# Two attentions in one kernel: the norms between them by groups of four tiles, and the second part's first-layer weights prepared inside the first attention

## What is computed

```
def core(x):                                   # x: (2, 1024, 128)
    x0 = layernorm(x)                          # norm 0
    a  = local_attention_1(x0)                 # 16 heads of 8, keys i-32..i, biases; one layer
    x  = x + layernorm(a)                      # norm 1 and the sum
    y  = layernorm(x)                          # norm 2
    for l in range(6):                         # 16 heads of 64, window 32, rotary tables
        y = y + attn_layer(shift(y), Wqkv[l], q_scale[l], k_scale[l], Wo[l])
        y = y + ffn_layer(shift(y), W1[l], W2[l])   # norm, gated GELU, hidden size 341
    return x + layernorm(y)                    # norm 3 and the last sum
```

## Time and profile before

| | |
|---|---|
| median of three executions | 2151.84 us (2143.28 to 2152.09) |
| profiled execution, its own time | 2149.59 us |
| span of its trace | 2147.8 us |
| busy share: TensorE, VectorE, ScalarE, GpSimd | 90%, 78%, 75%, 77% |
| opening, start of the span to the first attention | 24.2 us |
| first attention | 140.2 us |
| between it and the layers | 37.7 us |
| layers, up to the last `hidden` | 1921.0 us |
| from there to the end | 24.7 us |

### The profile page before, as it was taken

The page is one execution under the profiler, slowest core; times in us unless marked ns, Lnnn a source line. Parts: engine busy times, 40 slices in busy tenths (PEclk is TensorE's granted clock), DMA queues, the critical chain, the costliest instruction groups (busy, mean ns, idle before and its releaser), DMA issues.

```text
span 2147.8 us, 67396 instructions
## 1 busy us (share of the span) xinstructions
PE 1932.7 (90%) x22192; PEld 1460.9 (68%) x22192; DVE 1676.1 (78%) x4006; ACT 1604.5 (75%) x5607; POOL 1662.5 (77%) x1251
## 2 busy tenths in 40 slices
PE   5992999998999988999988999988999988999986
PEld 3761777774777774777774777774777774777772
DVE  4666888886888876888876888876888876988865
ACT  4872888884888874888884888874888885888872
POOL 2124999985999976899976899976899976999960
PEclk9995999999999999999999999999999999999998
DMA  2001321110311111211111211111211111112210
GB/s 63 13 12 50 82 55 44 44 45 25 88 44 44 44 45 38 76 44 44 44 45 41 74 44 44 44 45 42 73 44 44 44 45 35 46 44 49 54 28 20
DMA packets 44547, 99.43 MB, mean 46 GB/s; under 512 B 7344, under 2 KB 24208, under 8 KB 43504
## 3 DMA queue, kind: packets, MB, share of 16 engines
q1 hardware_dynamic: 44400, 97.59, 17.8%
HBM read 19.59 MB, written 1.05 MB: 10 GB/s over the span
## 4 chain that ended last, share of the span: by engine, by line
PE 27%; DVE 26%; issue 18%; ACT 18%; POOL 8%; DVEq 1%; POOLq 0%; ACTq 0%; DMA 0%; SPq 0%
ACT prob L485 10%; DVE n2c L791 6%; DVE n L784 5%; DVE ts_ L794 5%; ACT nat L501 4%; PE bank L1115 3%; PE bank L1149 3%; DVE tc_ L787 3%; DVE nmax L741 3%; PE bank L1122 3%; ACT kT L523 2%; PE bank L1151 2%; PE bank L1150 2%; POOL rn L319 2%; POOL ropeL L356 2%
## 5 line engine op out<-in xcount | busy, mean ns | idle before, releaser
L319 POOL TENSOR_TENSOR rn<-n2c,half_neg 128x8 f32<-128x8 f32 x384 | 632.8, 1648 | 129.5 <-DVE n2c L791 128.7
L485 ACT ACTIVATE prob<-bank,nmax 128x96 f32<-128x96 f32 x1536 | 504.1, 352 | 131.0 <-DVE nmax L741 130.8
L321 POOL TENSOR_TENSOR tsum<-tc_,ts_ 128x512 f32<-128x512 f32 x384 | 489.9, 1276 | 0.0
L324 POOL TENSOR_TENSOR w_nat<-tsum,rn 128x512 f32<-128x512 f32 x384 | 400.6, 1043 | 37.8 <-POOL tsum L321 15.1
L784 DVE TENSOR_REDUCE n<-nat 128x8 f32<-128x512 f32 x384 | 262.5, 683 | 140.9 <-ACT nat L501 138.2
L485 ACT ACTIVATION_READ_ACCUMULATOR prob<-bank,nmax 128x1 f32 x1536 | 334.3, 218 | 0.0
L1149 PE MATMUL bank<-w_hi,xs 128*128 128x512 f32 x576 | 277.0, 481 | 34.2 <-DVE ts_ L794 13.1
L494 ACT ACTIVATE pT<-bank 96x512 f32<-96x512 f32 x384 | 231.3, 602 | 74.4 <-PE bank L1122 72.3
L501 ACT ACTIVATE nat<-bank 128x512 f32<-128x512 f32 x384 | 233.0, 607 | 72.0 <-PE bank L1151 69.4
L794 DVE TENSOR_TENSOR ts_<-bank,ropeL 128x256 f32<-128x256 f32 x768 | 285.8, 412 | 0.0
L1122 PE MATMUL bank<-idf,prob 128*96 128x128 f32 x1536 | 244.9, 282 | 43.6 <-ACT kT L523 29.5
(11 more groups left out here) (125 smaller groups left out, 3413.7 us busy)
## 6 DMA issues: line engine op xcount, KB each, us to landing
vspace<-v_nat SPq DMA_DIRECT2D x96, 384.0 KB, 4.0
vspace<-v_nat SPq DMA_DIRECT2D x96, 256.0 KB, 3.4
vspace<-v_nat SPq DMA_DIRECT2D x95, 128.0 KB, 2.3
nat<-w_qkv SPq DMA_DIRECT2D x5, 1536.0 KB, 8.5
wo<-w_o SPq DMA_DIRECT2D x6, 512.0 KB, 4.0
w<-w SPq DMA_DIRECT2D x6, 341.0 KB, 3.0
shared<-w_qkv SPq DMA_DIRECT2D x1, 1536.0 KB, 6.8
w<-w SPq DMA_DIRECT2D x6, 192.0 KB, 3.0
```

Source lines behind the costliest of these rows:

```text
L319: nc.gpsimd.tensor_tensor(rn[:, r, :], n2c[:, r, :], half_neg[:, 0:8], ALU.pow).then_inc(pool_step, 1)
L321: nc.gpsimd.tensor_tensor(tsum[:, r, :], tc_[:, r, :], ts_[:, r, :], ALU.add).then_inc(pool_step, 1)
L324: nc.gpsimd.tensor_tensor(w_nat[:, r, :].rearrange("p (h d) -> p h d", d=D), tsum[:, r, :].rearrange("p (h d) -> p h d", d=D), rn[:, r, :] ...
L485: last = nc.scalar.activation(prob[:, 4 * b + i, :], SB[b][:, i * SPAN:(i + 1) * SPAN], ACT.Exp, bias=nmax[:, p, 8 * G + 4 * b + i:8 * G + ...
```

## The change

The four norms outside the layers are taken group by group. VectorE's part is split into `moments` (four `bn_stats`), `deviations` (four `bn_aggr`, and the addition) and `normalise` (four `tensor_scalar`), and GpSimd takes a power of four columns a group (`pow_norm`). The normalising of a group stands behind the next group's moments. TensorE transposes a group as soon as it is normalised. Each group of `x` has a semaphore of its own. The memsets have another order, with the four powers of norm 0 among them.

In the first attention VectorE takes the `bn_stats` of tile n - 1 inside tile n. SyncE issues layer 0's five weight loads before the attention. ScalarE does the three pieces of `split` in tiles 0, 1 and 14; GpSimd makes the four tables behind the keys of tiles 3, 5, 7 and 9, and two pieces of `rest` behind tiles 11 and 13 and the third after tile 15; its loop over tiles is written out.

At the end TensorE transposes groups 0 and 1 of the result before `down(3)`, VectorE takes their moments before `output(3)`, and the rest follows group by group.

```diff
-                              ).then_inc(x_loaded, 16)
+                              ).then_inc(x_in[s], 16)
...
+                    eng.dma_start(wqkv0, Wqkv[l, :, :]).then_inc(qkv_loaded, 16)
+                    eng.dma_start(wo[:, :, :], Wo[l, :, :].rearrange("(i p) c -> p i c", p=P)).then_inc(wo_loaded, 16)
+                    eng.dma_start(w1[:, :], W1[l, :, :]).then_inc(ffn_loaded, 16)
+                    eng.dma_start(w2[:, :, :], W2[l, :, :].rearrange("(i p) c -> p i c", p=P)).then_inc(ffn_loaded, 16)
+                    eng.dma_start(vec[:, :], par[l, :, :]).then_inc(ffn_loaded, 16)
...
-                    eng.wait_ge(phase, 4 * 2)
-                    eng.dma_start(wqkv0, Wqkv[l, :, :]).then_inc(qkv_loaded, 16)
...
+            def pow_norm(k, g):
+
+                eng.wait_ge(n_eps, k * SUPERS + g + 1)
+                nc.gpsimd.tensor_tensor(rstd[:, g * SUPER:(g + 1) * SUPER], veps[:, g * SUPER:(g + 1) * SUPER],
+                                        half_neg[:, 0:SUPER], ALU.pow).then_inc(n_pow, 1)
...
             nc.gpsimd.memset(half_neg[:, :], -0.5).then_inc(init_done, 1)
-            nc.gpsimd.memset(w_nat[:, :, :], 0.0).then_inc(init_done, 1)
-            nc.gpsimd.memset(kT[:, :, :, :], 0.0).then_inc(init_done, 1)
+            nc.gpsimd.memset(follows[:, :], 1.0).then_inc(init_done, 1)
             nc.gpsimd.memset(vw1[0:WIN, 0, 0, :], 0.0).then_inc(init_done, 1)
             nc.gpsimd.memset(xA[:, :, :], 0.0).then_inc(init_done, 1)
+            eng.wait_ge(init_done, 4)
+            nc.gpsimd.memset(follows[:, 0:TILES:PER_SEQ], 0.0).then_inc(init_done, 1)
+            pow_norm(0, 0)
+            pow_norm(0, 1)
+            nc.gpsimd.memset(kT[:, :, :, :], 0.0).then_inc(init_done, 1)
+            pow_norm(0, 2)
+            pow_norm(0, 3)
             nc.gpsimd.memset(xB[:, :, :], 0.0).then_inc(init_done, 1)
-            nc.gpsimd.memset(follows[:, :], 1.0).then_inc(init_done, 1)
-            eng.wait_ge(init_done, 7)
-            nc.gpsimd.memset(follows[:, 0:TILES:PER_SEQ], 0.0).then_inc(init_done, 1)
+            nc.gpsimd.memset(w_nat[:, :, :], 0.0).then_inc(init_done, 1)
             eng.wait_ge(init_done, 8)
-
-            def pow_rstd(k):
-
-                eng.wait_ge(ln_step, 2 * k + 1)
-                nc.gpsimd.tensor_tensor(rstd[:, :], veps[:, :], half_neg[:, :], ALU.pow).then_inc(ln_pow, 1)
 
             def rotate(q_idx):
...
-            pow_rstd(0)
...
-            split_keys(0, 0)
-            split_keys(1, 1)
-            with eng.Fori(1, TILES // 2) as i:
-                split_keys(i * 2, 0)
-                split_keys(i * 2 + 1, 1)
...
-            eng.wait_ge(c_loaded, CONSTS)
-            tables(0)
+
+            for t in range(TILES):
+                split_keys(t, t % 2)
+                if t in (3, 5, 7, 9):
+                    table(0, (t - 3) // 2)
+                if t in (11, 13):
+                    rest(0, (t - 11) // 2, True)
+            rest(0, 2, True)
             end(eng)
 
             begin(eng, 2)
-            pow_rstd(1)
-            rest(0, 0, True)
-            rest(0, 1, True)
-            pow_rstd(2)
-            rest(0, 2, True)
+            for k in (1, 2):
+                for g in range(SUPERS):
...
-            pow_rstd(3)
+            for g in range(SUPERS):
+                pow_norm(3, g)
...
                 if ahead:
                     qkv_first(t + 2, p)
                     copy_first(n + 3, 1 - p)
+                if isinstance(n, int) and n in (0, 1, TILES - 2):
+                    split(0, min(n, 2), True)
                 if not opening:
...
-            for k in range(3):
-                split(0, k, True)
...
+            def settle(last):
+
+                last.then_inc(n_step, 1)
+                steps[0] += 1
+                eng.wait_ge(n_step, steps[0])
...
+            def moments(src, g):
+                for n in range(g * SUPER, (g + 1) * SUPER):
                     last = nc.vector.bn_stats(stats[:, n, :], src[:, n, :])
-                last.then_inc(f_st, 1)
...
+            def deviations(g):
+                for n in range(g * SUPER, (g + 1) * SUPER):
                     last = nc.vector.bn_aggr(mv[:, n, :], stats[:, n, :])
-                last.then_inc(f_st, 1)
-                eng.wait_ge(f_st, fst[0])
-                fst[0] += 1
...
+            def normalise(src, k, g):
+                eng.wait_ge(n_pow, k * SUPERS + g + 1)
...
-            eng.wait_ge(x_loaded, 16 * SUPERS)
-            norms(x_nat, 0)
+            for g in range(SUPERS):
+                eng.wait_ge(x_in[g], 16)
+                moments(x_nat, g)
+                deviations(g)
+                if g:
+                    normalise(x_nat, 0, g - 1).then_inc(n_norm, 1)
+            normalise(x_nat, 0, SUPERS - 1).then_inc(n_norm, 1)
...
+                if not opening:
+                    eng.wait_ge(a_y, t)
+                    nc.vector.bn_stats(stats[:, n - 1, :], y_nat[:, n - 1, :])
...
+                eng.wait_ge(a_y, t + 1)
+                settle(nc.vector.bn_stats(stats[:, n, :], y_nat[:, n, :]))
...
-            norms(y_nat, 1)
-            eng.wait_ge(ln_step, 4)
-            nc.vector.tensor_tensor(x_nat[:, :, :], x_nat[:, :, :], ln_nat[:, :, :], ALU.add).then_inc(f_st, 1)
-            eng.wait_ge(f_st, fst[0])
-            fst[0] += 1
-            norms(x_nat, 2)
...
+            def add_up(g):
+
+                g4 = slice(g * SUPER, (g + 1) * SUPER)
+                settle(normalise(y_nat, 1, g))
+                settle(nc.vector.tensor_tensor(x_nat[:, g4, :], x_nat[:, g4, :], ln_nat[:, g4, :], ALU.add))
+                moments(x_nat, g)
+                deviations(g)
+
+            for g in range(SUPERS):
+                deviations(g)
+            for g in range(SUPERS):
+                add_up(g)
+                if g:
+                    normalise(x_nat, 2, g - 1).then_inc(n_norm, 1)
+            normalise(x_nat, 2, SUPERS - 1).then_inc(n_norm, 1)
             end(eng)
...
+            def final_moments(g):
+                eng.wait_ge(lnT_free, g + 1)
+                moments(y_nat, g)
+                deviations(g)
+
...
+                    if s == 3 and last:
+                        for g in range(2):
+                            final_moments(g)
...
+            def final_sum(g):
+                g4 = slice(g * SUPER, (g + 1) * SUPER)
+                settle(normalise(y_nat, 3, g))
+                nc.vector.tensor_tensor(x_nat[:, g4, :], x_nat[:, g4, :], ln_nat[:, g4, :], ALU.add).then_inc(out_ready, 1)
+
+            final_moments(2)
+            final_sum(0)
+            final_moments(3)
+            for g in range(1, SUPERS):
+                final_sum(g)
...
+            def transpose_norms(k):
+                for g in range(SUPERS):
+                    eng.wait_ge(n_norm, k * SUPERS + g + 1)
+                    transposes(lambda n: ln_nat[:, n, :], g)
+
+            def transpose_result(g):
+                eng.wait_ge(f_out, (DEPTH - 1) * SUPERS + g + 1)
+                transposes(lambda n: xA[:, n, 1:P + 1], g)
...
+                    elif last:
+                        transpose_result(0)
+                        transpose_result(1)
...
-            eng.wait_ge(f_out, DEPTH * SUPERS)
-            transposes(lambda n: xA[:, n, 1:P + 1], 2)
+            transpose_result(2)
+            transpose_result(3)
```

More of the change, by code:

```diff
@@ L973, in _ @@
             layers(eng, layer)
-            eng.wait_ge(lnT_free, SUPERS)
-            for n in range(TILES):
-                last = nc.vector.bn_stats(stats[:, n, :], y_nat[:, n, :])
-            last.then_inc(f_st, 1)
-            at = base_st + DEPTH * SUPERS
-            eng.wait_ge(f_st, at + 1)
-            for n in range(TILES):
-                last = nc.vector.bn_aggr(mv[:, n, :], stats[:, n, :])
-            last.then_inc(f_st, 1)
-            eng.wait_ge(f_st, at + 2)
-            nc.vector.tensor_scalar(veps[:, :], mv[:, :, 1], EPS, None, ALU.add).then_inc(ln_step, 1)
@@ L986, in _ @@
-            eng.wait_ge(ln_pow, 4)
-            for n in range(TILES):
-                last = nc.vector.tensor_scalar(ln_nat[:, n, :], y_nat[:, n, :], mv[:, n, 0:1], rstd[:, n:n + 1],
-                                               ALU.subtract, ALU.mult)
-            last.then_inc(f_st, 1)
-            eng.wait_ge(f_st, at + 3)
-            for s in range(SUPERS):
-                t4 = slice(s * SUPER, (s + 1) * SUPER)
-                nc.vector.tensor_tensor(x_nat[:, t4, :], x_nat[:, t4, :], ln_nat[:, t4, :], ALU.add).then_inc(out_ready, 1)
+            def final_sum(g):
+                g4 = slice(g * SUPER, (g + 1) * SUPER)
+                settle(normalise(y_nat, 3, g))
+                nc.vector.tensor_tensor(x_nat[:, g4, :], x_nat[:, g4, :], ln_nat[:, g4, :], ALU.add).then_inc(out_ready, 1)
@@ L997, in _, with transposes @@
+            final_moments(2)
[3 more added lines that the diff above has]
+                final_sum(g)
         @block.tensor
         def _(eng):
```

(12 more changed lines are left out.)

47 lines of the change are left out of this document (21 added, 26 removed).

## The result

The median after the change is 2129.93 us (2125.49 to 2131.05, five executions), against 2151.84 before. After over before is 0.990, with the interval 0.988 to 0.992: faster by 1.0%, where 2130.1 was forecast. The profiled execution took 2130.22 us with a span of 2128.4; before it was 2149.59 and 2147.8.

A forecast was written before the change was run, and what follows sets the result against it. The short stages were read as chains with one engine working at a time, most time lying in the untouched layers. Gains 3.3 - 1.3 + 13.1 + 6.6 = 21.7 us, from 2151.84 to 2130.1, range 2120 to 2140.

The forecast's parts named there:

- the table load starts at 16.6: Opening: ScalarE's table load waits for all eight memsets and starts at 16.6 instead of 19.87 us, gain 3.3 us.
- its lower end of 0: Opening: gain of 0 if the weight loads issued behind the constants delay these, for which TensorE waits.
- Tile 1's piece costs its full 0.96: First attention: split's piece in tile 1 stands right before ScalarE's copy of the heads, without slack, costing 0.96 us.
- Tiles 0 and 14: nothing: First attention: split's pieces cost 0, tile 14 having 1.63 us idle, tile 0 no such copy; tile 0's upper end 0.96.
- `bn_stats` fills the 0.27 us: First attention: VectorE's bn_stats, 0.22 us, fits its 0.27 us idle before a tile's third evacuation; 0.3 us in all.
- GpSimd's tables and SyncE's issues: nothing: First attention: tables and rest fit GpSimd's 6.63 us before the next keys, SyncE's issues precede the value moves; cost 0.
- the last power is not covered: 1.1: Between attention and layers: VectorE waits 1.1 us for GpSimd's last power before the last normalising.
- Rival 1: GpSimd's power also holds the port, so normalisings between and in the closing wait: 5 us less, 2135.1 us; chance 0.12.
- Rival 2: Moved work costs more: late constants, no opening gain, attention losing its upper bound of 3.5 us; 2135.6 us, chance 0.13.
- Rivals 3 and 4: GpSimd's pieces delay attention keys, 2146.4 us, chance 0.04; bn_stats makes VectorE the attention's bound, 2166.4 us, chance 0.02.
- the last store behind it stays: Closing: the last store after VectorE's last sum stays as before, within a gain of 6.6 us.
- the last store goes alone: Closing: upper end of the gain, 7.5 us, if the last store goes alone.

The follow-up runs named there:

- e8_between: Changed kernel with weight loads, split, tables and rest back where they stood before, norms by groups kept; median 2131.32 us, 0.9905 of before.
- e2_behind: Changed kernel with tile 1's piece of split moved behind ScalarE's copy of the heads; attention 140.78 us, one execution 2124.90 us.
- e1_late: Changed kernel with split's second and third pieces in tiles 14 and 15, second rest behind tile 15; attention 140.92 us, median 2124.24 us, 0.9896 of before.
- e3_half: Changed kernel with only half of split's second piece in tile 1, the other half in tile 15, second rest behind tile 15; attention 147.17 us, 2127.59 us.
- e5_memsets: Changed kernel with the memsets of xB and w_nat moved behind tile 1's keys; opening 18.82 us, one execution 2133.9 us.
- e9_best: Changed kernel with split pieces in tiles 14 and 15, identity's own semaphore, xB and w_nat memsets behind tile 1's keys, vspace memset before the powers; 2122.41 us.
- e6_idf: Changed kernel with TensorE's first transposes waiting for the identity alone, by its own semaphore; opening 19.00 us, one execution 2125.96 us.
- e7_idf_mem: Changed kernel with the identity's own semaphore and the xB and w_nat memsets behind tile 1's keys; opening 16.37 us, one execution 2120.36 us.

## Why the prediction was right, and where it was not

**The frame held.** The reading that the short stages are chains in which one engine works at a time on all 16 tiles was right, and it carries the result: the two stages that were counted along VectorE's chain gave 23.1 us, and 19.7 were forecast. `e8_between` shows that the groups bring it. The total of 21.7 was 2.3 above the 19.4 of the profiles, within 0.2 us of the difference of the medians. That closeness is luck in part: +1.1, -3.2, +1.9, -3.6 and +1.5 cancel.

**The opening** gained 4.4 instead of 3.3, by another path than the one argued. The step "the table load starts at 16.6", behind the eighth memset, failed: it started at 15.50, before that memset's end, and in `e2_behind` at 14.07. Only the first copy waits (15.79 there). So the load and the wait overlap, and by the memset alone the stage would end at 16.0 + 3.1 = 19.1. But in this profile another wait ended last, TensorE's for the constants: 14.30 + 5.5 = 19.8. The text had named late constants as its lower end of 0, and TensorE waiting for them as a sign of being wrong; that wait came, 1.9 us later than before in this profile, and cost 0.7. The hold by GpSimd's memset of `kT`, set at 0.7, is there (1.07 us for `veps`).

**The first attention** cost 4.5 instead of 1.3, outside the given 3.5. The terms one by one:
- *Tile 1's piece costs its full 0.96*: that held, 0.95 us in front of the copy of the heads and 1.09 of TensorE's idle time in front of the projection, and none in `e2_behind`. What the sum left out is what TensorE does behind the wait: the clock fell to 1.2 GHz and stayed there for about 6.8 us, with 32 small matmuls at 1.88 us that take 1.11 at the full clock. That is a term of its own, 3.03 us, put at nothing without being named. Both together are 3.98.
- *Tiles 0 and 14: nothing.* Tile 14 took 7.16 us from the copy of the heads ahead of its piece to the copy behind it, and 7.17 before. For tile 0 no cost shows: from the attention's start to the values of tile 1 it took 20.99 us, 0.65 less than before, and 20.88 in `e8_between`, without the piece. But this stretch varies by more than that with the clock.
- *`bn_stats` fills the 0.27 us*: it takes 0.28 in front of the third evacuation, and the eleven tiles in the middle took 86.79 us instead of 86.42. That is 0.03 each, 0.4 in all where 0.3 was forecast.
- *The end* took 0.8 more from tile 15's copy of the heads on. It does so too in `e2_behind` and `e8_between` (8.72 and 8.86 us, against 7.80 before), but not in `e1_late` (7.84). At this end TensorE's clock goes down in all kernels as its work runs out, and the sooner it does so behind that copy, the longer the step, in all twelve profiles: 8.88 us with the fall 0.5 us behind the copy (`e3_half`), 8.58 with 0.9 (after), 8.17 with 1.4 (`e5_memsets`), 7.80 with 1.9 (before) and 7.58 with 2.2 (`e9_best`). So these 0.8 us are a price of the clock too. What moves the fall was not tried.
- *GpSimd's tables and SyncE's issues: nothing.* Confirmed: the keys came in time, and `e1_late` with all transfers in place took 140.92 us, where `e8_between`, without them, took 140.80; the eleven tiles in the middle took 86.76 and 86.77. So the weights' transfers do not slow the attention.

Added up: 0.95 and 3.03 in tile 1, 0.4 in the middle and 0.8 at the end, less 0.65 at the start, are the 4.5.

How far the fall of the clock follows from the piece: it fell behind tile 1 in five of seven profiles with a piece or half of one in front of the copy, and in none of five without. In the two exceptions (`e6_idf`, `e7_idf_mem`) TensorE was as idle, and the clock stayed. The windows of `e7_idf_mem`:

```profile
38.00:40.00 2.00, 0.92 (x10) 0.28 (x6) 0.43 (x1) 2.00 (x7) 2.00 (x2) 1.00 0.18 41
40.00:44.00 4.00, 4.00 (x60) 3.52 (x59) 3.14 (x7) 4.00 (x27) 0.57 (x1) 1.00 0.02 4
```

and its timeline:

```profile
37.99 0.28 ACT L471 ACTIVATE v_nat<-bank 128x128 f32<-128x128 f32 x1 [1.34 <-DMA vspace<-v_nat]
...
39.81 0.46 PE L1099 MATMUL bank<-vspace,oT 128*128 128x128 f32 x2 [1.08 <-ACT oT L487]
...
46.79 0.28 ACT L471 ACTIVATE v_nat<-bank 128x128 f32<-128x128 f32 x1 [1.46 <-DMA vspace<-v_nat]
```

There o0 to o1 took 7.85, as without a piece, but v to v took 8.80 (8.79 in `e6_idf`) in place of 7.88 in `e1_late`: the wait in front of the copy is not made up for, and is the 0.95 that the prediction gave it. So the piece costs 0.95 us in every profile that has it there whole, and the clock 3.0 more in most of them and not in all. What sets it off besides the idle time stays open; the two kernels without the fall differ from the kernel after in the opening (and `e7_idf_mem` in two memsets behind tile 1's keys), and two profiles are few.

**Between** gained 15.0 instead of 13.1, above its upper end. The step "the last power is not covered: 1.1" failed: it is covered by the normalising of group 2 (182.32 beside 182.49), and the sum had counted both. The memset of `vspace` held VectorE by about 0.4, not 0.95: 2.76 against 2.35 for eight. A step of `add_up` with a normalising behind it came to 4.28 instead of 4.4, 0.4 us over the stage. The start and the undisturbed eight took 0.3 more than counted, and the end, from VectorE's last normalising to the layers, the 2.1 of the forecast. (The text's own bounds, 202.1 and 188.9, give 13.2 and not 13.1.)

**Rival 1**, the power as a lock, is refuted: 1.11 us for four normalisings right beside a power of 1.03 us, here and in the closing. The Trainium skill (SBUF — State Buffer, "Who interferes with whom") says that whichever of the two engines issues first has the shared port pair for its whole instruction, and the other is blocked. Subtraction (1.62 us for four columns in `e8_between`) and memset (1.07 in `e7_idf_mem`) behave so here, the power does not. Whether that lies in the operation or in its size stays open: the powers beside VectorE had 4 columns, or 8, the subtraction and the memsets 1024 and more, and no run has a wide power or a narrow subtraction there. Rival 2 had its two parts: the constants were late, and the attention passed its upper bound, by a mechanism that it did not name. Their price, 5.5 us together, did not come, since the opening still gained. Rivals 3 and 4 did not come about: no keys were late, and VectorE did not become the bound of a tile.

**The closing** gained 8.1 instead of 6.6. The last sum ended 13.9 us after the last `hidden` (14.4 forecast). The rest is the store: from the last sum to the end of the span it took 2.7 us, where the step "the last store behind it stays" kept 3.7. Each store carries a quarter of the result (256 KB) in both kernels. Before, four were issued within 2.3 us and took 2.4 to 3.2 us to land; now they are spread over 7.0 us and take 2.3 each. That is the text's own upper end, "the last store goes alone".

**The layers** were put at nothing, and took 3.6 us more in these two profiles. The instructions are the same, and two edits of the changed kernel (`e3_half`, `e7_idf_mem`) lie below the 1921.0 of before. Over 1920.4 to 1928.5 in twelve profiles this can't be told from spread.

## What to carry to other kernels

A chain of whole-array steps on one engine is worth its other engines' idle time when it is cut into groups: counting the chain instruction by instruction from rows of the same trace came within 2 us of 15 here; the last group's link to another engine is covered by the group before it, so count it once. When small work is put into a loop that TensorE bounds, look at the one instruction behind which TensorE waits, and put the work behind it and not in front: a piece of 1 us there cost that 1 us, and 3 us more where the clock fell behind it, and the same instruction one step later cost nothing. And where a stage has two late events, removing one of them gains next to nothing; name both before either is priced.

## What the runs showed of the hardware

- GpSimd's power of four columns beside VectorE's `tensor_scalar` costs neither of them anything that shows (1.11 beside 1.03 us; 1.11 and 1.01 alone), while GpSimd's subtraction and memset, of 1024 columns and more, hold even a `tensor_scalar` of four columns, 1.62 and 1.07 us against 0.17 undisturbed.
- ScalarE's table load waited for TensorE's bank, but ran ahead of the wait for the memset that held its copy: it started at 14.07 in `e2_behind` and the copy at 15.79, with the awaited memset ending at 15.75.
- Around a hole of 0.67 to 2.03 us in TensorE's work, in an otherwise dense stretch, its granted clock went from 1.00 to 0.50 in five profiles; in two, with holes of 1.08, it stayed at 1.00.
- Identical instructions, the six layers, took 1920.4 to 1928.5 us in twelve profiles: 8.1 us or 0.4%, where the change gained 19.4 in its profile.
